# A local-attention stage on Trainium2: the mask moves from TensorE to VectorE, the output projection takes two tiles at a time, and the feed-forward moves between the halves of the weighing

## The chip, the cores and the metric

One Trainium2 chip, one of its cores. The metric is the device time of one execution of the whole program in microseconds; lower is better. The program runs nine phases one after the other. The change touches one of them, the local transformer, which takes from about 486 to 3685 us.

## The reference, cut to what matters

The input x is eight sequences of 512 tokens with 128 features. The local transformer has six layers, each an attention of 16 heads of 64 in windows of 32 keys with one window of look-back, and a gated feed-forward of 341 hidden units:

```
def local_attention(q, k, v):        # w = 32, bk2 = previous window and own window
    mask = (it < jb) | (it > jb + w) | (jb == -1)
    sim = jnp.einsum('bhwie,bhwje->bhwij', bq, bk2) * QK_SCALE
    sim = jnp.where(mask, -jnp.finfo(sim.dtype).max, sim)
    attn = jax.nn.softmax(sim, -1)
    out = jnp.einsum('bhwij,bhwje->bhwie', attn, bv2)
    return out.reshape(b, h, n, d)
...
    q = l2norm(q) * qs
    k = l2norm(k) * ksc
    q = q * cos * scale + rotate_half(q) * sin * scale
    k = k * cos * inv + rotate_half(k) * sin * inv
    return out @ Wo
...
for i in range(DEPTH):               # DEPTH = 6
    x = attn_layer(shift_tokens(x), Wqkv[i], q_scale[i], k_scale[i], Wo[i]) + x
    x = ffn_layer(shift_tokens(x), ln_g[i], ln_b[i], W1[i], b1[i], W2[i], b2[i]) + x
```

All is float32. Before this phase stands a gated delta rule; behind it follow a causal attention, a mixture of experts, a chunked attention, a second mixture of experts, another attention and a third mixture.

## The kernel before, in words

**Tiles.** A tile is 128 tokens; four tiles (t = k mod 4 = 0 to 3) are a sequence, 32 tiles a layer, 192 tiles the phase. Each engine has its own program in `local_transformer_phase`, unrolled in Python over `k` from -2 to 199, with semaphores counted per tile or per sequence; nothing is planned at run time, the order of the calls in each engine's loop is the order of the work. In iteration k the engines work on several tiles at once: the softmax and weighing of tile k, values and turned q and k of tile k+1, the q and k projections of tile k+2, the output of tile k-1.

**PE (loop at L1350).** make_scores(k): two bf16 matmuls write the mask into the two score banks (identity times `band8`, L1207), then 128 small matmuls of 64 rows and 32 columns add the scores on top (L1214). Then project_v (L1186 to L1188, three matmuls per 512 columns, float32 split in two parts), project_qk(k+2, 0), turn_out(k-1) (L1277), project_qk(k+2, 1), turn_probs(k) (L1253, waits for the exponentials), turn_qk(k+1) (L1266), weigh_values(k, 0), project_out(k-1) (L1304: eight 128x128 float32 products, each of two instructions in the trace), weigh_values(k, 1) (L1292, 64 small matmuls each half), and then the feed-forward's share: t = 0 ffn_a (L1342), t = 1 ffn_out (L1347) and ffn_turn (L1320), t = 3 ffn_gate (L1336). make_scores(k) waits for the first half of att of tile k-1 (`att_ready`).

**DVE (loop at L1674).** centre(k): maximum over each window from PSUM (L1605), subtraction of it from PSUM into `scores` (L1608). products(k+2): q and k times the rotary tables (L1618, four operations). sum_squares (L1624, one after the products and one after the first divide), ffn_shift at t = 2, divide(k, 0) and divide(k, 1) (L1630, L1634), between them add_output(k-1) (L1641). Then ffn_products at t = 0, ffn_add and ffn_stats at t = 1 (L1669, L1646 to L1653).

**ACT (loop at L1484).** invert_norms, copy_v, square(k+2, 0) (L1422), exponentials(k) (L1410), copy_out(k-1), square(k+2, 1), copy_probs, two copy_qk; scale_norm ahead of the square at t = 3, gelus with two table loads behind everything at t = 3.

**POOL (loop at L1560).** At t = 2 invert_deviation first (L1556, waits for the statistics); then normalise(k+1), two operations of 128x1024 with both inputs in SBUF (L1551), rotate(k+2), four of 128x512 (L1541), guard_norms.

**SP** issues the copies of the windows of v (window_values) and the weights of the next layer.

**PSUM** is full: scores and probabilities share banks 0 and 1, values, turned output and output projection (`WO_BANK`) banks 2 and 3, turned q and k banks 2 to 5, q and k 4 to 7, the feed-forward 6, 7 and 3. The waits `after_qk` and `ffn_banks_read` keep them apart.

## Time and profile before

| | us |
|---|---|
| median of 3 runs | 4785.16 |
| lowest and highest | 4783.14, 4789.26 |
| profiled execution | 4791.83 |
| its span, first to last instruction | 4789.8 |
| mean granted TensorE clock (share of full) | 0.927 |

Busy time of the whole span: PE 4238.3 us, the weight loads beside it (PEld) 3371.5, DVE 3247.4, ACT 2600.4, POOL 2418.3. Busy time says how long an engine had an instruction at work; on PE instructions overlap, so start-to-start times in the timeline are read rather than durations. In the timeline each line is one group of instructions alike: start, time, engine, line of the kernel, operation, what is written and read, the count, and in brackets how long the engine had been idle and who released it. "issue" means that the profile shows nothing that the engine waited for.

### The profile page before, as it was taken

Reading aid. Unit: us, or ns where it says so; the run is one execution under the profiler, and the core shown is the slowest. Engines: PE = TensorE matmul, PEld = TensorE weight load, DVE = VectorE, ACT = ScalarE, POOL = GpSimd, SP = SyncE. Lnnn points to the kernel's source line nnn. Section 1 sums busy time; section 2 is a strip of 40 time slices with the busy share of each in tenths; the row PEclk is TensorE's granted clock in tenths of the full one; section 3 lists DMA queues with packets and bytes.
Section 4 is the critical chain, followed back from the end, with each engine's and each line's share of the span. In section 5 each row is a group of like instructions: output and inputs, shape, how many; then the busy total and the mean of one; then the engine's idle time right before and its main releaser. Section 6 shows DMA issues by size and latency. Waiting matters only on the chain. (4 is left out here: it accounts for less than half of the span.)

```text
span 4789.8 us, 167679 instructions
## 1 busy us (share of the span) xinstructions
PE 4238.3 (88%) x70890; PEld 3371.5 (70%) x70890; DVE 3247.4 (68%) x5510; ACT 2600.4 (54%) x4233; POOL 2418.3 (50%) x1949
## 2 busy tenths in 40 slices
PE   6997899999999999999999999999997749658667
PEld 5885777777777777777777777777775439558447
DVE  4445777777777777777777777777775564564554
ACT  2231566665666666666666666666664317546435
POOL 2123655656565566555565666555652037516025
PEclk9777999999999999999999999999998959868878
DMA  0000322222222322222222222222221021222022
GB/s 25 0 0 30 88 67 65 64 80 67 69 67 62 86 66 69 64 80 69 69 64 80 68 64 70 64 69 69 69 64 36 0 61 50 67 61 62 7 63 75
DMA packets 214200, 281.53 MB, mean 59 GB/s; under 512 B 58878, under 2 KB 103716, under 8 KB 212740
## 3 DMA queue, kind: packets, MB, share of 16 engines
q1 hardware_dynamic: 203972, 251.85, 19.9%
q0 software_dynamic: 9536, 19.55, 1.5%
q8 instruction: 545, 8.93, 0.8%
q14 instruction: 147, 1.20, 0.1%
HBM read 54.88 MB, written 18.28 MB: 15 GB/s over the span
## 5 line engine op out<-in xcount | busy, mean ns | idle before, releaser
L1541 POOL TENSOR_TENSOR local_normed<-local_rot,local_sines 128x512 f32<-128x512 f32 x768 | 953.8, 1276 | 818.4 <-PE local_bank L1266 813.9
L1551 POOL TENSOR_TENSOR local_normed<-local_normed,local_inv_norm 128x1024 f32<-128x1024 f32 x384 | 732.8, 1929 | 276.1 <-ACT local_inv_norm L1441 276.1
L1618 DVE TENSOR_TENSOR local_rot<-local_bank,local_table 128x1024 f32<-128x1024 f32 x384 | 470.3, 1225 | 409.2 <-ACT local_squares L1422 402.6
L1186 PE MATMUL local_bank<-local_wqkv_hi,local_ys_hi 128*128 128x512 f32 x1152 | 496.8, 431 | 28.4 <-issue 17.4
L1417 ACT COPY local_v_tile<-local_bank 128x1024 f32<-128x1024 f32 x192 | 195.1, 1016 | 548.0 <-PE local_bank L1188 548.0
L1618 DVE TENSOR_TENSOR local_sines<-local_bank,local_table 128x1024 f32<-128x1024 f32 x384 | 466.4, 1215 | 0.0
L1624 DVE TENSOR_REDUCE local_norm<-local_squares 128x16 f32<-128x1024 f32 x384 | 464.0, 1209 | 0.0
L1188 PE MATMUL local_bank<-local_wqkv_hi,local_ys_lo 128*128 128x512 f32 x1152 | 458.8, 398 | 0.0
L1187 PE MATMUL local_bank<-local_wqkv_lo,local_ys_hi 128*128 128x512 f32 x1152 | 456.5, 396 | 0.0
L1422 ACT ACTIVATE local_squares<-local_bank 128x1024 f32<-128x1024 f32 x384 | 396.9, 1034 | 78.7 <-PE local_bank L1188 78.7
L1605 DVE TENSOR_REDUCE local_top<-local_bank 128x16 f32<-128x1024 f32 x192 | 234.8, 1223 | 246.2 <-PE local_bank L1214 245.8
L1304 PE MATMUL local_bank<-local_att_t,local_wo 128*128 128x128 f32 x3072 | 390.2, 280 | 4.3 <-ACT local_att_t L1446 1.2
L1304 PEld LDWEIGHTS local_bank<-local_att_t,local_wo 128*128 128x128 f32 x3072 | 358.6, 192 | 29.9 <-issue 9.9
L1266 PE MATMUL local_bank<-ident,local_normed 128*128 128x128 f32 x3072 | 373.7, 275 | 4.8 <-POOL local_normed L1551 4.1
L1292 PE MATMUL local_bank<-local_vals,local_probs_t 64*32 64x65 f32 x24576 | 348.2, 225 | 23.9 <-issue 20.6
L1266 PEld LDWEIGHTS local_bank<-ident,local_normed 128*128 128x128 f32 x3072 | 333.7, 142 | 24.5 <-POOL local_normed L1551 5.4
L1214 PEld LDWEIGHTS local_bank<-local_k_t,local_q_t 64*32 64x32 f32 x24576 | 256.7, 105 | 130.2 <-issue 129.9
L1292 PEld LDWEIGHTS local_bank<-local_vals,local_probs_t 64*32 64x32 f32 x24576 | 273.7, 105 | 90.7 <-issue 66.3
L1214 PE MATMUL local_bank<-local_k_t,local_q_t 64*32 64x64 f32 x24576 | 292.8, 225 | 43.9 <-issue 43.9
L1186 PEld LDWEIGHTS local_bank<-local_wqkv_hi,local_ys_hi 128*128 128x128 f32 x1152 | 220.6, 192 | 78.9 <-issue 30.7
L1634 DVE TENSOR_TENSOR local_att<-local_bank,local_inv_sum 128x512 f32<-128x512 f32 x384 | 265.5, 691 | 13.2
L1188 PEld LDWEIGHTS local_bank<-local_wqkv_hi,local_ys_lo 128*128 128x128 f32 x1152 | 220.2, 191 | 51.6
(421 smaller groups left out, 8957.0 us busy)
## 6 DMA issues: line engine op xcount, KB each, us to landing
local_vals<-local_v_tile SPq DMA_DIRECT2D x1152, 130.0 KB
local_vals<-local_v_tile SPq DMA_DIRECT2D x672, 65.0 KB
local_stage<-in_L_ffn_Wqkv SPq DMA_DIRECT2D x6, 1536.0 KB
moe_w<-y_rows SPq DMA_DIRECT2D x32, 256.0 KB, 4.9
moe_w<-in_L_ffn_W SPq DMA_DIRECT2D x3, 2048.0 KB, 9.9
x_rows<-moe_rows SPq DMA_DIRECT2D x12, 512.0 KB, 3.9
local_wo<-in_L_ffn_Wo SPq DMA_DIRECT2D x6, 512.0 KB, 9.0
moe_taken<-x_rows,moe_take POOLq DMA_INDIRECT x149, 2.6
```

Source lines behind the costliest of these rows:

```text
L1186: nc.tensor.matmul(out, hi, wqkv_hi[:, d0:d1], start=True, stop=False)
L1187: nc.tensor.matmul(out, hi, wqkv_lo[:, d0:d1], start=False, stop=False)
L1188: return nc.tensor.matmul(out, lo, wqkv_hi[:, d0:d1], start=False, stop=True)
L1214: last = nc.tensor.matmul(bank[b * BLOCK:(b + 1) * BLOCK, SCORES[odd], c * WIN:(c + 1) * WIN], q_t[rows, c, b * BLOCK:(b + 1) * BLOCK], k_ ...
L1266: last = nc.tensor.transpose(bank[:, QK_TURN[a][j // 4], j % 4 * P:(j % 4 + 1) * P], normed[:, (8 * a + j) * P:(8 * a + j + 1) * P], g.ide ...
L1292: last = nc.tensor.matmul(bank[b * BLOCK:(b + 1) * BLOCK, WEIGHED[i][odd], j * (HD + 1):(j + 1) * (HD + 1)], probs_t[rows, c, b * BLOCK:(b ...
L1304: last = nc.tensor.matmul(bank[:, WO_BANK, 0:P], wo[:, c, :], att_t[:, c, :], start=(c == 0), stop=(c == CH - 1))
L1422: nc.scalar.activation(squares[:, a * INNER:(a + 1) * INNER], two(QK[a]), ACT.Square).then_inc(q["squared"], 1)
L1541: last = nc.gpsimd.tensor_tensor(of_heads(normed, a)[:, :, to], of_heads(rot, a)[:, :, to], of_heads(sines, a)[:, :, of], ALU.add)
L1551: nc.gpsimd.tensor_tensor(of_heads(normed, a), of_heads(normed, a), inv_norm[:, a * HEADS:(a + 1) * HEADS].unsqueeze(2).to_broadcast([P, H ...
L1618: last = nc.vector.tensor_tensor(of_heads(out, a), src, table[:, m % TILES, row, :].unsqueeze(1).to_broadcast([P, HEADS, HD]), ALU.mult)
L1624: nc.vector.tensor_reduce(norm2[:, cols], of_heads(squares, a), AX, ALU.add).then_inc(q["norms_ready"], 1)
```

## The change

The two mask matmuls leave make_scores, and `band8` and `ident16` with them; the scores' matmuls start their own banks. centre adds the mask on VectorE while it copies the scores out of PSUM, takes the maximum from SBUF and subtracts in place. project_out runs in even iterations only, for the two tiles k-2 and k-1, with 256 moving columns; add_output likewise. `att_t` is twice as wide, and copy_out fills its half. PE's ffn_out, ffn_turn and ffn_gate move from behind weigh_values(k, 1) to before it, with a new wait `after_turn`; weigh_values(k, 1) comes behind them. Semaphore targets follow (`last_pair` is the last odd tile up to m, `wo_done` and `y_added` count two at once).

```diff
 def make_scores(m):
-    for odd in range(2):
-        nc.tensor.matmul(bank[:, SCORES[odd], :], ident16[:], band8[:, min(t, 1)].rearrange("p h k -> p (h k)"),
-                         start=True, stop=False, skip_group_check=True)
...
-                        start=False, stop=True, skip_group_check=True, tile_position=(HD * odd, b * BLOCK))
+                        start=True, stop=True, tile_position=(HD * odd, b * BLOCK))
 def project_v(m, k):
-    pe.wait_ge(q["y_added"], tile("y_added", k - 2))
+    pe.wait_ge(q["y_added"], tile("y_added", last_pair(k - 2)))
 def project_out(m):
-        last = nc.tensor.matmul(bank[:, WO_BANK, 0:P], wo[:, c, :], att_t[:, c, :], start=(c == 0), stop=(c == CH - 1))
-    last.then_inc(q["wo_done"], 1)
+        last = nc.tensor.matmul(bank[:, WO_BANK, 0:2 * P], wo[:, c, :], att_t[:, c, :], start=(c == 0), stop=(c == CH - 1))
+    last.then_inc(q["wo_done"], 2)
+def after_turn(k):
+    if is_tile(k + 1):
+        pe.wait_ge(q["qkt_copied"], tile("qkt_copied", k + 1, 1))
 def ffn_gate(n, k):
     after_qk(k)
+    after_turn(k)
 def ffn_out(n, k):
+    after_turn(k)
 # PE's loop
     if is_tile(k):
         weigh_values(k, 0)
-    if is_tile(k - 1):
+    if is_tile(k - 1) and k % 2 == 0:
         project_out(k - 1)
-    if is_tile(k):
-        weigh_values(k, 1)
-    if t == 0 and is_seq(n - 2):
-        ffn_a(n - 2, k)
     if t == 1 and is_seq(n - 2):
         ffn_out(n - 2, k)
     if t == 1 and is_seq(n - 1):
         ffn_turn(n - 1, k)
     if t == 3 and is_seq(n - 1):
         ffn_gate(n - 1, k)
+    if is_tile(k):
+        weigh_values(k, 1)
+    if t == 0 and is_seq(n - 2):
+        ffn_a(n - 2, k)
 # ACT
 def copy_out(m):
-    nc.scalar.copy(att_t[:].rearrange("p c t -> p (c t)"), two(OUT_TURN)).then_inc(q["out_copied"], 1)
+    nc.scalar.copy(att_t[:, :, m % 2 * P:(m % 2 + 1) * P], two(OUT_TURN).rearrange("p (c t) -> p c t", t=P)).then_inc(q["out_copied"], 1)
 # DVE
 def centre(m):
+    rows = scores[:].rearrange("p c a k -> p a c k")
     dve.wait_ge(q["scores_done"], tile("scores_done", m))
-    nc.vector.tensor_reduce(top[:], src, AX, ALU.max).then_inc(q["max_ready"], 1)
+    dve.wait_ge(q["probs_turned"], tile("probs_turned", m - 1))
+    nc.vector.tensor_tensor(rows, src, band[:, min(m % TILES, 1)].unsqueeze(1).unsqueeze(1).to_broadcast([P, 2, CH, WIN]),
+                            ALU.add).then_inc(q["masked"], 1)
+    dve.wait_ge(q["masked"], tile("masked", m))
+    nc.vector.tensor_reduce(top[:], rows, AX, ALU.max).then_inc(q["max_ready"], 1)
     dve.wait_ge(q["max_ready"], tile("max_ready", m))
-    dve.wait_ge(q["probs_turned"], tile("probs_turned", m - 1))
-    nc.vector.tensor_tensor(scores[:].rearrange("p c a k -> p a c k"), src, top[:].unsqueeze(3).to_broadcast([P, 2, CH, WIN]),
+    nc.vector.tensor_tensor(rows, rows, top[:].unsqueeze(3).to_broadcast([P, 2, CH, WIN]),
                             ALU.subtract).then_inc(q["centred"], 1)
 def add_output(m):
-    y = g.XH[:, s, c0:c0 + P]
-    nc.vector.tensor_tensor(y, bank[:, WO_BANK, 0:P], y, ALU.add).then_inc(q["y_added"], 1)
+    y = g.XH[:, s, c0:c0 + 2 * P]
+    nc.vector.tensor_tensor(y, bank[:, WO_BANK, 0:2 * P], y, ALU.add).then_inc(q["y_added"], 2)
```

## Rows read from the trace of the kernel before

**Rows 1.** The page: busy time by engine, and the instruction queue's packets and MB.
```profile
PE 4238.3 (88%) x70890; PEld 3371.5 (70%) x70890; DVE 3247.4 (68%) x5510; ACT 2600.4 (54%) x4233; POOL 2418.3 (50%) x1949
...
q8 instruction: 545, 8.93, 0.8%
```
**Rows 2.** Busy time by window: each engine's us and instructions, granted clock, DMA.
```profile
1700.00:2200.00 500.00, 482.26 (x9962) 374.71 (x9962) 382.65 (x511) 307.95 (x417) 300.87 (x236) 0.99 0.27 70
```
**Rows 3.** Timeline of PE, tile with t = 1, cut to its stations.
```profile
2220.15 0.59 PE L1207 MATMUL local_bank<-local_band,local_ident 128*128 128x512 bf16 x2
2220.68 1.48 PE L1214 MATMUL local_bank<-local_k_t,local_q_t 64*32 64x64 f32 x128
...
2227.24 1.04 PE L1253 MATMUL local_bank<-ident,local_scores 128*128 128x128 f32 x8
...
2230.03 0.86 PE L1292 MATMUL local_bank<-local_vals,local_probs_t 64*32 64x65 f32 x64
2230.90 2.02 PE L1304 MATMUL local_bank<-local_att_t,local_wo 128*128 128x128 f32 x16
2232.86 0.86 PE L1292 MATMUL local_bank<-local_vals,local_probs_t 64*32 64x65 f32 x64
2233.65 2.85 PE L1347 MATMUL local_bank<-local_gates,local_w 128*128 128x512 f32 x6
2236.42 0.46 PE L1320 MATMUL local_bank<-ident,XH 64*128 64x64 f32 x8
2236.82 0.61 PE L1207 MATMUL local_bank<-local_band,local_ident 128*128 128x512 bf16 x2
```
**Rows 4.** PE: starts of one sequence, its t = 3, the next; L1207 over the stage.
```profile
2203.84 0.59 PE L1207 MATMUL local_bank<-local_band,local_ident 128*128 128x512 bf16 x2
...
2250.80 0.59 PE L1207 MATMUL local_bank<-local_band,local_ident 128*128 128x512 bf16 x2 [0.40 <-DVE local_att L1634]
...
2268.08 0.59 PE L1207 MATMUL local_bank<-local_band,local_ident 128*128 128x512 bf16 x2
...
L1207 PE MATMUL local_bank<-local_band,local_ident x384: 376/379/391, 486.0 to 3635.7; 128*128 128x512 bf16 x192
```
**Rows 5.** Timeline of DVE in the same tile (t = 1) and into the next.
```profile
2222.20 1.23 DVE L1605 TENSOR_REDUCE local_top<-local_bank 128x16 f32<-128x1024 f32 x1 [1.03 <-PE local_bank L1214]
...
2226.20 1.22 DVE L1618 TENSOR_TENSOR local_rot<-local_bank,local_table 128x1024 f32<-128x1024 f32 x1 [1.52 <-ACT local_squares L1422]
...
2231.25 1.21 DVE L1624 TENSOR_REDUCE local_norm<-local_squares 128x16 f32<-128x1024 f32 x1
...
2236.53 0.75 DVE L1669 SCALAR_TENSOR_TENSOR XH<-local_bank,local_ln,XH 128x512 f32<-128x512 f32 x1 [1.07 <-PE local_bank L1347]
2237.61 0.87 DVE L1646 BATCH_NORM_STATS2 local_stats<-local_y_tok 128x6 f32<-128x128 f32 x4 [0.33 <-ACT local_y_tok L1452]
...
2239.01 1.22 DVE L1605 TENSOR_REDUCE local_top<-local_bank 128x16 f32<-128x1024 f32 x1
```
**Rows 6.** Timeline of ACT in the same tile: the square and the exponentials.
```profile
2225.14 1.03 ACT L1422 ACTIVATE local_squares<-local_bank 128x1024 f32<-128x1024 f32 x1 [0.35 <-PE local_bank L1188]
2226.06 1.05 ACT L1410 ACTIVATE local_scores<-local_scores 128x1024 f32<-128x1024 f32 x1
```
**Rows 7.** DVE's L1599 by its line (ns, least, median, most); POOL's timeline at t = 2.
```profile
L1599 DVE TENSOR_TENSOR local_wqkv_lo<-local_stage,local_wqkv_hi x18: 1214/2919/2922, 460.4 to 3117.0; 128x1024 fp32r<-128x1024 f32 x18
...
2239.18 1.04 POOL L1556 TENSOR_TENSOR local_rstd<-local_var_eps,minus_half 128x4 f32<-128x4 f32 x1 [1.97 <-DVE local_var_eps L1653]
2240.19 3.77 POOL L1551 TENSOR_TENSOR local_normed<-local_normed,local_inv_norm 128x1024 f32<-128x1024 f32 x2
```
**Rows 8.** PE's waits, 700 to 3500 us: total us, times, longest.
```profile
PE local_bank L1214 <- issue: 34.8, 22, 2.1
```
**Rows 9.** Timeline of PE: stops in the scores, first tiles and one at t = 3.
```profile
502.87 0.31 PE L1214 MATMUL local_bank<-local_k_t,local_q_t 64*32 64x64 f32 x5 [1.55 <-issue]
...
562.92 0.63 PE L1214 MATMUL local_bank<-local_k_t,local_q_t 64*32 64x64 f32 x37 [1.42 <-issue]
...
2319.56 0.27 PE L1214 MATMUL local_bank<-local_k_t,local_q_t 64*32 64x64 f32 x2 [1.76 <-issue]
```
**Rows 10.** Busy time by window behind that stop; the clock is third from the end.
```profile
2315.00:2325.00 10.00, 7.83 (x183) 6.03 (x179) 5.25 (x7) 3.88 (x9) 5.08 (x4) 0.83 0.03 8
```

More of the change, by code:

```diff
@@ L1024, in body @@
         band = sb("band", [P, 2, WIN])
-        band8 = sb("band8", [P, 2, CH, WIN], BF16)
-        ident16 = sb("ident16", [P, P], BF16)
         squares = sb("squares", [P, 2 * INNER])
@@ L1043, in body @@
         att = sb("att", [P, INNER])
-        att_t = sb("att_t", [P, CH, P])
+        att_t = sb("att_t", [P, CH, 2 * P])
         y_tok = sb("y_tok", [P, TOKENS])
@@ L1058, in body @@
                     "exp_done": 1, "v_copied": 1, "squared": 2, "probs_t_ready": 1, "qkt_copied": 2, "out_copied": 1,
-                    "max_ready": 1, "centred": 1, "qk_normed": 2, "products_ready": 2, "norms_ready": 2,
+                    "masked": 1, "max_ready": 1, "centred": 1, "qk_normed": 2, "products_ready": 2, "norms_ready": 2,
                     "sums_inverted": 2, "att_ready": 2, "y_added": 1,
@@ L1075, in body @@
                     "logs_ready", "inv_norms_ready")
-        DVE_MADE = ("max_ready", "centred", "products_ready", "norms_ready", "sums_inverted", "att_ready", "y_added",
+        DVE_MADE = ("masked", "max_ready", "centred", "products_ready", "norms_ready", "sums_inverted", "att_ready", "y_added",
                     "stats_ready", "aggregated", "var_ready", "shift_ready", "prod_ready", "seq_done")
@@ L1104, in is_seq, with last_pair @@
             return 0 <= n < RUNS
+        def last_pair(m):
+            return m if m % 2 else m - 1
         def two(banks):
@@ L1181, in _ @@
                 credit(pe, PE_MADE)
-                pe.wait_ge(pads_ready, 2)
+                pe.wait_ge(pads_ready, 1)
                 def product(out, hi, lo, d0, d1):
@@ L1273, in turn_out @@
                     else:
-                        pe.wait_ge(q["y_added"], tile("y_added", m - 1))
+                        pe.wait_ge(q["y_added"], tile("y_added", last_pair(m - 1)))
                         ffn_banks_read(k - 1, (3,))
@@ L1297, in project_out @@
                 def project_out(m):
-                    if m % PER_LAYER == 0:
+                    if m % PER_LAYER == 1:
                         pe.wait_ge(wo_loaded, 16 * (m // PER_LAYER + 1))
@@ L1444, in copy_out @@
                     act.wait_ge(q["out_turned"], tile("out_turned", m))
-                    act.wait_ge(q["wo_done"], tile("wo_done", m - 1))
-                    nc.scalar.copy(att_t[:].rearrange("p c t -> p (c t)"), two(OUT_TURN)).then_inc(q["out_copied"], 1)
+                    act.wait_ge(q["wo_done"], tile("wo_done", last_pair(m - 1)))
+                    nc.scalar.copy(att_t[:, :, m % 2 * P:(m % 2 + 1) * P], two(OUT_TURN).rearrange("p (c t) -> p c t", t=P)).then_inc(q["out_copied"], 1)
                 def copy_turned(n):
@@ L1478, in _ @@
                 nc.scalar.preload_act_table_set("natural_log_exp_and_others")
-                act.wait_ge(pads_ready, 2)
+                act.wait_ge(pads_ready, 1)
                 for part in range(3):
@@ L1581, in _ @@
                 dve.wait_ge(consts_loaded, CONST_LOADS)
-                nc.vector.tensor_copy(ident16[:], g.ident[:])
-                nc.vector.tensor_copy(band8[:], band[:].unsqueeze(2).to_broadcast([P, 2, CH, WIN])).then_inc(pads_ready, 1)
                 def scale_tables(layer):
@@ L1637, in add_output @@
                 def add_output(m):
-                    s, c0 = m // TILES % SEQS, m % TILES * P
+                    s, c0 = m // TILES % SEQS, (m - 1) % TILES * P
                     dve.wait_ge(q["wo_done"], tile("wo_done", m))
-                    y = g.XH[:, s, c0:c0 + P]
-                    nc.vector.tensor_tensor(y, bank[:, WO_BANK, 0:P], y, ALU.add).then_inc(q["y_added"], 1)
+                    y = g.XH[:, s, c0:c0 + 2 * P]
+                    nc.vector.tensor_tensor(y, bank[:, WO_BANK, 0:2 * P], y, ALU.add).then_inc(q["y_added"], 2)
                 def ffn_stats(n):
@@ L1687, in _ @@
                         sum_squares(k + 2, 1)
-                    if is_tile(k - 1):
+                    if is_tile(k - 1) and k % 2 == 0:
                         add_output(k - 1)
```

## The prediction

> **What bounds the kernel now.** I read the page first: PE is the busiest engine, 88% of the span [rows 1]. The busy share by windows then shows the stage that the diff touches, the local transformer (about 486 to 3685 us, 192 tiles): PE 482 of 500 us, DVE 383, ACT 308, POOL 301 [rows 2]. The timeline of PE shows one tile as an unbroken run: mask 0.53 us (start to start), scores 1.41, projections and the turned output to 6.56 after the scores' start, then the turned probabilities, the turned q and k, the first half of the weighing at 9.35, project_out 1.96, the second half 0.79, then the feed-forward's share of that tile [rows 3]. Four tiles (t = 0 to 3) make one sequence: the one shown takes 64.24 us [rows 4], and I take 63.9 for one with no stop at all. Over the stage the mask's line gives the mean: 3149.7 us for 191 tiles, 65.96 a sequence [rows 4]. PE waits for another engine at one place in each sequence, 0.40 us for DVE's att ahead of t = 3 [rows 4]. So PE's order sets the time, and whoever is late with the softmax comes next.
>
> I write S for the start of a tile's scores (2220.68). From [rows 5, 6]: DVE begins the max at S+1.52 and has centred at S+4.0; ACT does a square at S+4.46 and only then the exponentials at S+5.38, which end as PE reaches turn_probs (S+6.56). The centring has 1.4 us of slack, turn_probs has none.
>
> **What the change takes from PE.**
> Mask: 4 x 0.53 = 2.1 us a sequence; the scores' own 128 products stay [rows 3].
> project_out: two tiles took 2 x 1.96 = 3.92. The new form has 16 instructions of 256 columns for the pair. Those of 512 columns start every 0.45 us (2.77 us for 6, L1347) and those of 128 every 0.12 (1.96 for 16) [rows 3], so 256 lies near 0.22 and the pair near 3.5. Bounds: 3.9 (no gain at all) and 2.0 (as dear as one tile was). I take 3.5, nearest to half the 512 form: 0.8 us a sequence.
> Wait for att: the odd tiles get the feed-forward between the halves, the even ones 3.5 us of projection, so att's first half has over 1 us of slack: 0.4 us goes.
> Sum on PE alone: 63.9 - 3.3 = 60.6 us a sequence. (The two DVE operations that made the bf16 tables once, before the loop, go as well: under 2 us, left out.)
>
> **What it adds.**
> (a) The add is one 128x1024 VectorE operation. No such row from PSUM plus a table exists except L1618 (1.22, PSUM times a table) [rows 5]: 1.25 us with its gap, bounds 1.1 and 1.9. The max then reads SBUF, as L1624 does in 1.21. If DVE is free, centring ends at S+5.25 instead of 4.0, and the exponentials can't start before S+5.38 anyway. So the add costs nothing in a tile where DVE is free and alone; each us later than that is one us of PE.
> (b) The subtraction now has both inputs in SBUF. The row for that is L1599, 1.21 us at least and 2.92 at the median of 18 [rows 7]: it is the same size, and its long cases lie beside POOL's normalising (L1551, 1.9 each). The difference, 1.7, is nearly one POOL operation. So I price a meeting by what is left of POOL's running operation, 0 to 1.9 us. (The Trainium skill, "SBUF — State Buffer", section "Who interferes with whom", says that a VectorE instruction with two SBUF inputs contends with a GpSimd instruction that reads SBUF, that the loser is fully blocked, and that a reduce never contends; the trace agrees with the first part by 2.92 against 1.21. By the rule the new max is safe and the subtraction is not.)
> (c) t = 2. During t = 1 DVE has, after the second att, ffn_add and the statistics: L1669, L1646 and their small followers take 0.67 + 1.40 us to the next max [rows 5]. PE's t = 1 is now only 9.35 + 0.88 + 2.77 + 0.40 + 0.83 = 14.2 us (it was 16.67, with mask and project_out in it). DVE: the first norm sum at S+10.57 [rows 5] plus 1.13, att 0.84, second sum 1.13: 13.7; it waits for the second half of the weighing to 14.35; att to 15.2, ffn_add 15.9, statistics 17.25. PE's scores of t = 2 start at 14.2 and DVE would be wanted at 15.7: 1.5 us late. POOL's deviation and normalising follow the statistics (1.01 us apart) [rows 7]: 18.4 to 20.3 for the first half; the subtraction comes at 19.75 and waits 0.55. Exponentials 2.0 us late, PE idle 2.0 us ahead of turn_probs of t = 2. Bounds: 1.5 (no meeting) and 3.4 (a whole POOL operation).
> (d) Other tiles. t = 3: the normalising is in its second half when the subtraction comes, 0.65 us, hidden by the 0.6 that scale_norm puts ahead of the exponentials there. t = 0: 0.2. t = 1: POOL is done by then, 0.
> (e) ffn_gate stands 0.88 us after the start of the weighing and waits for products_ready of the tile after next (after_qk); the products end about 0.5 us later: 0.5 us in t = 3. Behind it the second half of the weighing waits too. ffn_turn has ffn_out's 2.77 us as cover and waits for nothing. SP's queue is not reordered; its window copies hang on pv_done of the second half, now up to 1.2 us later in odd tiles after the first, needed a tile later. ACT's gelus start earlier, their table loads lie in the gap that was idle.
> Result: t = 0 17.3 + 0.2, t = 1 14.2, t = 2 14.6 + 2.0, t = 3 14.3 + 0.5, together 63.1 against 63.9: only 0.8 of the 3.3 us is left, 46 sequences x 0.8 = 37 us.
>
> (f) The stop for instructions. Twenty-two times in the stage PE stops inside the scores for "issue", 34.8 us in all [rows 8]. The page has 545 packets on the instruction queue for 141,780 PE and PEld instructions: about 260 each [rows 1]. By counting instructions along the timeline, the stops lie a multiple of 256 apart. In the steady state all are at t = 3, and only where such a boundary lies in the second half of the scores: t = 3 is the one tile whose scores come right after 64 weighing products, with no feed-forward (12 slow instructions in 2.7 us) between. The first tiles, which have none either, stop in each of five: 1.55, 0.45, 1.64, 0.18 and 1.42 us, mean 1.05 (first and last of them shown) [rows 9]. After the change the scores come right behind the second half of the weighing in three of four tiles, and the mask's 0.53 us between is gone. At t = 2 DVE is 1.5 us late anyway and hides most of it. At t = 3 and t = 0: 2 x (1.05 + 0.3 for the lost mask at half the boundaries) = 2.7 us a sequence, against 34.8/43 = 0.8 now: 1.9 more, 87 us. Bounds: 0 (other lateness takes them in) and 3.2 a sequence (2.4 us, the longest kind, at half the boundaries of all three, less what DVE hides).
> (g) After 8 of those 22 stops the granted clock fell: a stretch of 10 us shows 0.83 [rows 10] and eight matmuls at 0.43 instead of 0.23 us; that is about 1.8 us each. Twice the stops: 0.35 a sequence, 16 us. Bounds 0 and 50.
> (h) Five layer boundaries, where the DVE is behind by its weight splits: 1.25 to 3 us each, 8 us.
>
> **Sum.** -37 + 87 + 16 + 8 = +74 us. The profiled execution took 4791.8 us (span 4789.8), so 4866 for its like; its median sister runs are 6.7 us lower, 4785.2, so I forecast 4859.
>
> **Rivals.**
> B, the stops don't multiply: boundaries still come, but the other waits of the new order cover them. For it: they are absent in every tile with a feed-forward between, so the queue refills in under 3 us. Against it: the stops of the first tiles [rows 9]. Time: 4785 - 37 + 8 = 4756; with project_out at its best, about 4700. This is the case on the other side, and the point where it decides is whether "issue" ahead of the scores stays near 35 us; up to about 70 us it still comes out level or faster.
> C, PE stays the bound and DVE's additions are hidden at t = 2 too (statistics earlier than I set them, no meeting with POOL): 4785 - 46 x 3.3 = 4633, and up to 4700 with the 0.5 of ffn_gate and some stops. Against it: DVE's work in t = 1 alone adds up to more than PE's tile.
> D, stops at full price in all three tiles and the clock falls after many of them and after the 2 us waits of t = 2: 87 becomes 147, 16 becomes 50: 4785 - 37 + 147 + 50 + 8 = 4953.
> That project_out gains nothing would move each of these by 46 x 0.8 = 37 us and is in the ranges. The change does what it says in all of them: the mask's lines can't be hidden work on PE.
>
> **How the numbers follow.** Forecast 0.42 (4800 to 4910), B 0.22, C 0.14, D 0.22. The likeliest is 4859. The range leaves out the lower half of C and the far end of D: 4690 to 4950. A measurement of this kernel can tell about 0.2% (10 us) from no change. Faster: C and most of B, 0.34; within 0.2%: the seam between B and the forecast, 0.06; slower 0.60.
>
> **What would show it.** Right: no L1207 matmul; the pair's projection at 3.4 to 3.6 us per 16 instructions; VectorE's add at 1.2; the subtraction with a median near 1.2 and a tail to 3 us; PE waiting some 2 us for ACT's scores ahead of turn_probs in every fourth tile; "issue" ahead of the scores' products over 100 us. Wrong: "issue" unchanged (then B), turn_probs never waiting (then C), or the mean sequence under 65 us.

## The result, and the profile after

The changed kernel takes 4842.99 us (median of 4 runs, 4836.72 to 4844.17), the kernel before 4787.21 beside it: ratio 1.0107, 95% interval 1.0089 to 1.0125, so 1.1% slower. The profiled execution has a span of 4842.4 us against 4789.8. In the local stage the scores of the first and of the last of its 192 tiles start at 483.7 and 3686.7 us, 3203.0 us apart; in before they start at 486.5 and 3636.0, 3149.5 apart. So the whole difference of the spans, 52.6 us, lies in that stage.

The page of after, the share by windows (as [rows 2]) and PE's waits from 700 to 3500 us (total us, times, longest; as [rows 8]):

```profile
PE 4138.4 (85%) x68970; PEld 3281.9 (68%) x68970; DVE 3574.1 (74%) x5604; ACT 2599.8 (54%) x4233; POOL 2453.6 (51%) x1949
...
q8 instruction: 530, 8.68, 0.8%
```

```profile
1700.00:2200.00 500.00, 460.05 (x9607) 354.94 (x9592) 430.25 (x521) 299.81 (x406) 300.22 (x233) 0.99 0.25 67
```

```profile
PE local_bank L1213 <- issue: 90.8, 58, 2.4
PE local_bank L1252 <- ACT local_scores L1416: 48.9, 51, 3.1
PE local_bank L1341 <- DVE local_sines L1625: 25.9, 40, 0.7
PE local_bank L1188 <- issue: 20.9, 10, 4.0
PE local_bank L1276 <- ACT local_v_tile L1423: 11.8, 22, 1.0
```

PE has 100 us less work over the span and yet fills only 460 of 500 us, where it filled 482. What it saves it spends waiting: for instructions inside the scores (90.8 us, 34.8 before), for the exponentials ahead of the turned probabilities (48.9, 4.0 before), and ahead of ffn_gate for the products (25.9, none before). Two waits of before are gone: stops for instructions inside the weighing (18.0 us) and the wait for att (9.9). The same view of before, behind the 34.8 us of [rows 8]:

```profile
PE local_bank L1292 <- issue: 18.0, 43, 1.6
...
PE local_bank L1207 <- DVE local_att L1634: 9.9, 25, 0.4
PE local_bank L1253 <- ACT local_scores L1410: 4.0, 5, 0.9
```

PE's timeline, two tiles with t = 0 and what stands between, cut to its stations (as [rows 3, 4]):

```profile
2161.30 1.26 PE L1213 MATMUL local_bank<-local_k_t,local_q_t 64*32 64x64 f32 x105
2163.97 0.42 PE L1213 MATMUL local_bank<-local_k_t,local_q_t 64*32 64x64 f32 x23 [1.41 <-issue]
...
2169.47 1.03 PE L1252 MATMUL local_bank<-ident,local_scores 128*128 128x128 f32 x8
...
2173.14 3.69 PE L1303 MATMUL local_bank<-local_att_t,local_wo 128*128 128x256 f32 x16
2176.76 0.86 PE L1291 MATMUL local_bank<-local_vals,local_probs_t 64*32 64x65 f32 x64
2177.55 2.84 PE L1347 MATMUL local_bank<-local_xn,local_w 128*128 128x512 f32 x6
2180.32 1.49 PE L1213 MATMUL local_bank<-local_k_t,local_q_t 64*32 64x64 f32 x128
...
2194.32 1.08 PE L1213 MATMUL local_bank<-local_k_t,local_q_t 64*32 64x64 f32 x87
2197.49 0.66 PE L1213 MATMUL local_bank<-local_k_t,local_q_t 64*32 64x64 f32 x41 [2.08 <-issue]
...
2224.24 2.81 PE L1341 MATMUL local_bank<-local_xn,local_w 128*128 128x512 f32 x6 [0.65 <-DVE local_sines L1625]
2226.99 0.86 PE L1291 MATMUL local_bank<-local_vals,local_probs_t 64*32 64x65 f32 x64
2227.64 1.01 PE L1213 MATMUL local_bank<-local_k_t,local_q_t 64*32 64x64 f32 x79
2229.20 0.73 PE L1213 MATMUL local_bank<-local_k_t,local_q_t 64*32 64x64 f32 x49 [0.55 <-issue]
...
2235.72 1.09 PE L1252 MATMUL local_bank<-ident,local_scores 128*128 128x128 f32 x8 [0.54 <-ACT local_scores L1416]
...
2246.64 1.48 PE L1213 MATMUL local_bank<-local_k_t,local_q_t 64*32 64x64 f32 x128
```

Look at the two t = 0 tiles. The first stops for 1.41 us and then doesn't wait for the exponentials; the second stops for 0.55 and waits 0.54. They take 19.02 us (2161.30 to 2180.32) and 19.00 (2227.64 to 2246.64). The stop and the late softmax lie in the same stretch, and the tile takes as long as the longer of them asks. Why the softmax is late there is on the other engines, DVE and then POOL and ACT, in the second of these tiles:

```profile
2229.97 1.23 DVE L1610 TENSOR_TENSOR local_scores<-local_bank,local_band 128x1024 f32<-128x1024 f32 x1 [1.15 <-PE local_bank L1213]
2231.23 1.22 DVE L1613 TENSOR_REDUCE local_top<-local_scores 128x16 f32<-128x1024 f32 x1
2232.48 2.09 DVE L1615 TENSOR_TENSOR local_scores<-local_scores,local_top 128x1024 f32<-128x1024 f32 x1
```

```profile
2229.72 3.77 POOL L1557 TENSOR_TENSOR local_normed<-local_normed,local_inv_norm 128x1024 f32<-128x1024 f32 x2 [2.23 <-ACT local_inv_norm L1447]
```

```profile
2234.61 1.06 ACT L1416 ACTIVATE local_scores<-local_scores 128x1024 f32<-128x1024 f32 x1 [0.66 <-DVE local_scores L1615]
```

The add and the maximum take 1.23 and 1.22 us. The subtraction takes 2.09. It starts 0.9 us after the second of POOL's two operations has started and ends 1.08 us after that one has ended (2234.57 and 2233.49). In a t = 0 tile without a stop (scores from 2296.00) it starts 0.15 us into the second operation, takes 2.83, and ends 1.07 after it:

```profile
2300.09 2.83 DVE L1615 TENSOR_TENSOR local_scores<-local_scores,local_top 128x1024 f32<-128x1024 f32 x1
```

```profile
2298.08 3.77 POOL L1557 TENSOR_TENSOR local_normed<-local_normed,local_inv_norm 128x1024 f32<-128x1024 f32 x2 [2.23 <-ACT local_inv_norm L1447]
```

In the tile with the stop of 1.41 us it starts 1.75 us into the second operation and takes 1.24, and ends 1.08 us after it too. So POOL's end sets the subtraction's end, whether PE has stopped for 0, 0.55 or 1.41 us, and that is how a stop hides. From the third sequence on the t = 0 tiles with stops up to 1.4 us take 18.97 to 19.30 us, as those without one do; the eight with stops above 1.8 us take 19.63 to 21.67. The line over all tiles (ns: least, median, most) shows the meeting as the prediction set it out, one of 1.2 us alone and up to 3.0 when it waits:

```profile
L1615 DVE TENSOR_TENSOR local_scores<-local_scores,local_top x192: 1224/1227/2970, 488.3 to 3692.4; 128x1024 f32<-128x1024 f32 x192
```

Length of a tile, from the start of its scores (in before of its mask) to the next (us; from the third sequence on, layer boundaries left out). "Least" is the shortest tile, one without a stop for instructions; I call such tiles quiet. It can hold other waits:

| t | before, least / mean | predicted without stops | after, least / mean |
|---|---|---|---|
| 0 | 16.17 / 16.35 | 17.5 | 18.97 / 19.28 |
| 1 | 16.67 / 16.87 | 14.2 | 13.97 / 14.02 |
| 2 | 13.96 / 14.08 | 16.6 | 16.39 / 16.97 |
| 3 | 16.79 / 18.31 | 14.8 | 14.87 / 16.07 |
| sum | 63.6 / 65.6 | 63.1 | 64.2 / 66.3 |

With the boundaries a sequence takes 67.16 us in the mean against 66.27.

### The profile page after: what moved, and what is told of

Same layout as the page of the kernel before. It is cut to its first block and busy times, and to the rows that moved or that the text cites. A ratio compares the mean times of both kernels' runs of the same rounds, so it can differ in the third digit from the quotient of the medians.

```text
span 4842.4 us, 163981 instructions
## 1 busy us (share of the span) xinstructions
PE 4138.4 (85%) x68970; PEld 3281.9 (68%) x68970; DVE 3574.1 (74%) x5604; ACT 2599.8 (54%) x4233; POOL 2453.6 (51%) x1949
## 3 DMA queue, kind: packets, MB, share of 16 engines
q14 instruction: 149, 1.22, 0.1%
## 5 line engine op out<-in xcount | busy, mean ns | idle before, releaser
L1557 POOL TENSOR_TENSOR local_normed<-local_normed,local_inv_norm 128x1024 f32<-128x1024 f32 x384 | 767.9, 2021 | 169.5 <-ACT local_inv_norm L1447 169.5
L1625 DVE TENSOR_TENSOR local_rot<-local_bank,local_table 128x1024 f32<-128x1024 f32 x384 | 469.5, 1223 | 185.9 <-ACT local_squares L1428 179.0
L1213 PE MATMUL local_bank<-local_k_t,local_q_t 64*32 64x64 f32 x24576 | 307.2, 226 | 112.7 <-issue 108.6
L1265 PE MATMUL local_bank<-ident,local_normed 128*128 128x128 f32 x3072 | 378.6, 277 | 5.0 <-POOL local_normed L1557 4.1
L1213 PEld LDWEIGHTS local_bank<-local_k_t,local_q_t 64*32 64x32 f32 x24576 | 268.4, 105 | 158.2 <-issue 156.0
L1303 PE MATMUL local_bank<-local_att_t,local_wo 128*128 128x256 f32 x1536 | 354.9, 384 | 2.6 <-ACT local_att_t L1452 1.1
L1265 PEld LDWEIGHTS local_bank<-ident,local_normed 128*128 128x128 f32 x3072 | 338.6, 143 | 25.4 <-POOL local_normed L1557 5.6
L1610 DVE TENSOR_TENSOR local_scores<-local_bank,local_band 128x1024 f32<-128x1024 f32 x192 | 235.0, 1224 | 155.1 <-PE local_bank L1213 154.7
L1291 PE MATMUL local_bank<-local_vals,local_probs_t 64*32 64x65 f32 x24576 | 332.7, 225 | 5.5 <-issue 2.2
L1615 DVE TENSOR_TENSOR local_scores<-local_scores,local_top 128x1024 f32<-128x1024 f32 x192 | 314.6, 1638 | 6.6
L1303 PEld LDWEIGHTS local_bank<-local_att_t,local_wo 128*128 128x128 f32 x1536 | 283.9, 190 | 50.2 <-issue 1.7
```

Of the source, the lines that this page charges most:

```text
L1213: last = nc.tensor.matmul(bank[b * BLOCK:(b + 1) * BLOCK, SCORES[odd], c * WIN:(c + 1) * WIN], q_t[rows, c, b * BLOCK:(b + 1) * BLOCK], k_ ...
L1265: last = nc.tensor.transpose(bank[:, QK_TURN[a][j // 4], j % 4 * P:(j % 4 + 1) * P], normed[:, (8 * a + j) * P:(8 * a + j + 1) * P], g.ide ...
L1291: last = nc.tensor.matmul(bank[b * BLOCK:(b + 1) * BLOCK, WEIGHED[i][odd], j * (HD + 1):(j + 1) * (HD + 1)], probs_t[rows, c, b * BLOCK:(b ...
L1303: last = nc.tensor.matmul(bank[:, WO_BANK, 0:2 * P], wo[:, c, :], att_t[:, c, :], start=(c == 0), stop=(c == CH - 1))
L1557: nc.gpsimd.tensor_tensor(of_heads(normed, a), of_heads(normed, a), inv_norm[:, a * HEADS:(a + 1) * HEADS].unsqueeze(2).to_broadcast([P, H ...
L1625: last = nc.vector.tensor_tensor(of_heads(out, a), src, table[:, m % TILES, row, :].unsqueeze(1).to_broadcast([P, HEADS, HD]), ALU.mult)
```

## The experiments

They ran on three chips (e1 to e4, e5 to e8, e9 to e12), each time with the kernel before beside them. On the first of these chips the kernel before takes 4900 us, on the others 4791, so each kernel is given as its ratio to before on its own chip, and set against 1.0107 for after, which was not run again on them. The profiled executions allow a second comparison. Behind the last tile's scores 1263 to 1269 us follow on the chip of e1 to e4 and 1149 to 1164 on the others, so that chip is slower behind the stage. The stage itself, first to last tile's scores, takes 3149.5 us in before, 3203.0 in after, 3148.9 in e1, 3202.1 in e2, 3279.3 in e3, 3144.4 in e4, 3218.3 in e5 and 3153.6 in e6: the same picture as the ratios, to within 0.3% of the time.

**e1, the mask back on TensorE** (pair and new order kept):

```
-  dve: rows = src + band;  top = max(rows);  rows = rows - top
+  pe:  for odd in range(2): matmul(bank[:, SCORES[odd], :], ident16, band8[:, min(t, 1)], start=True, stop=False)
+  dve: top = max(src);  rows = src - top
```

> The changed kernel with the mask back on TensorE (two bf16 matmuls ahead of the scores) and the maximum and subtraction reading PSUM again; pair projection and new order stay. Theory (late softmax at t = 0 and t = 2 from VectorE's add and the meeting with POOL, plus more stops for instructions): PE gets 2.1 us a sequence back to do, but both lates go and the 0.53 us gap returns; near 4785 us, waits of turn_probs for ACT under 5 us, stops in the scores still some 60. Rival (the new order and its stops alone cost the time, the add is free): not faster than the changed kernel, 4845 to 4940 us, since PE only gets more work.

Measured: 1.0018 (1.0009 to 1.0028). Nearly the whole loss is gone. Least lengths 17.92, 14.63, 15.24 and 15.54: t = 0 and t = 2 win 1.1 us each, t = 1 and t = 3 lose 0.7 each. PE's waits:

```profile
PE local_bank L1218 <- issue: 60.5, 55, 1.7
PE local_bank L1346 <- DVE local_sines L1629: 27.5, 42, 0.7
...
PE local_bank L1257 <- ACT local_scores L1421: 3.9, 5, 0.8
```

The wait for the exponentials goes from 48.9 to 3.9 us. The stops are nearly as many (55 for 58), but 1.1 us each instead of 1.6, shorter by about the 0.53 us that the mask's two products take between the weighing and the scores.

**e2, the old order** (feed-forward's pieces again behind the second half of the weighing; mask and pair as in after):

```
-                    if t == 1: ffn_out, ffn_turn;  if t == 3: ffn_gate
                     weigh_values(k, 1)
+                    if t == 1: ffn_out, ffn_turn;  if t == 3: ffn_gate
```

> The changed kernel with ffn_out, ffn_turn and ffn_gate behind the second half of the weighing again. Theory: only t = 3 has its scores right behind the weighing, so stops in the scores fall from 60 to about 22; the 0.65 us waits of ffn_gate for VectorE's products go; VectorE is still late at t = 2 and meets POOL at t = 0. Near 4800 us. Rival (order is harmless, the add on VectorE is all of the loss): same as the changed kernel, 4843, stops unchanged.

Measured: 1.0123 (1.0106 to 1.014), no better than after. Near 4800 us were expected, hardly any loss; that was a miss:

```profile
PE local_bank L1291 <- ACT local_k_t L1440: 69.9, 84, 0.8
PE local_bank L1252 <- ACT local_scores L1416: 42.1, 73, 2.2
PE local_bank L1213 <- issue: 34.2, 25, 2.3
PE local_bank L1291 <- issue: 33.9, 30, 1.6
```

The stops in the scores fall to 34.2 us, what before had. But in the odd tiles, which have no projection any more, the second half of the weighing now stands right behind the first and waits 0.8 us for ACT's copy of k, and stops for instructions itself. The new order is what fills the place that the pairing left empty; the two edits belong together, and undoing one of them shows a wait that neither before nor after has.

**e3, one tile's projection at a time** (mask and order as in after):

```
-                    if is_tile(k - 1) and k % 2 == 0: project_out(k - 1)      # 256 columns
+                    if is_tile(k - 1):                project_out(k - 1)      # 128 columns
```

> The changed kernel with one tile of output projection per iteration again (128 moving columns). Theory: PE does 0.3 to 0.8 us more a sequence, but t = 1 gets 1.96 us longer and VectorE's statistics are done in time for t = 2, so the lateness there shrinks from 1.9 to at most a meeting: 4800 to 4850 us, about the same as the changed kernel. Rival (pairing is a plain gain of PE time, nothing hangs on it): 4843 + 37 = 4880.

Measured: 1.0252 (1.0235 to 1.0269), 1.4% over after, beyond both expectations. So the pairing is worth about 1.5 us a sequence, not 0.8. PE's own part is smaller than that: the pair starts at 2173.14 and the next block at 2176.76, so it takes 3.62 us against 2 x 1.96 [rows 3], which is 0.6 a sequence. The medians of t = 1 and t = 3 lose 1.8 and 2.3 us, while t = 0 and t = 2 win back only 1.3 and 1.1 of the 1.66 (3.62 - 1.96) that their shorter projection saves. What holds these two back was not followed to its end.

**e4, the maxima in PSUM**, so that the subtraction has one input in SBUF:

```
+                    top = bank[:, PROBS[0], 0:2 * CH].rearrange("p (a c) -> p a c", c=CH)
-                    nc.vector.tensor_reduce(top[:], rows, AX, ALU.max)        # top: a tensor in SBUF
+                    nc.vector.tensor_reduce(top, rows, AX, ALU.max)
```

> The changed kernel with the window maxima written to PSUM (bank 0, free once the add has read the scores), so that the subtraction has one SBUF input only; the same computation. Theory: the subtraction takes 1.22 us in every tile (mean now 1.64), POOL's normalising 1.90 (now 2.02); t = 0 falls from 19.0 to near 17.3 us where no stop falls into it, t = 2 by 0.5; about 4790 us. Rival (the subtraction's long times are waits that cost nothing, because stops and statistics are late anyway): 4835 to 4845, same as the changed kernel.

Measured: 1.0021 (1.0009 to 1.0034), 0.9% below after. The subtraction's line and PE's waits:

```profile
L1615 DVE TENSOR_TENSOR local_scores<-local_scores,local_bank x192: 1220/1220/1223, 491.1 to 3637.6; 128x1024 f32<-128x1024 f32 x192
```

```profile
PE local_bank L1212 <- issue: 94.1, 62, 2.2
...
PE local_bank L1251 <- ACT local_scores L1415: 17.2, 20, 2.1
```

The same 128x1024 operation at the same places takes 1220 ns each of 192 times; the least t = 0 tile falls from 18.97 to 17.52 us, which is what was predicted for it. POOL's normalising gains too: 2024 ns in the mean of after, 1932 before, 1934 here. (The Trainium skill, "SBUF — State Buffer", section "Who interferes with whom", has it so: one SBUF input doesn't contend with GpSimd, two do, and the reduce never does. The trace agrees: beside POOL the subtraction took up to 2970 ns with two SBUF inputs and at most 1223 with one, and the reduce from SBUF at most 1223 in after.)

**e5, the statistics later**: ffn_stats behind the softmax's three operations in t = 2 instead of ahead of them, and the deviation behind POOL's normalising.

```
                     if is_tile(k): centre(k)
+                    if t == 2: ffn_stats(n - 1)
...
-                    if t == 1: ffn_stats(n - 1)
```

> After, with the statistics of the feed-forward's normalisation issued behind the centring on VectorE in t=2, and the deviation's inverse behind the normalisation on the other engine, so that t=2's maximum and subtraction no longer stand behind them. Theory (the softmax of t=2 is late because VectorE does the statistics first): t=2 falls from 16.4 us to about 14.6 to 15.0, the time to some 1% below after (ratio to before near 1.002 instead of 1.0107). Rival (t=2 is late because the maximum waits for the scores themselves and the subtraction meets POOL, the statistics only fill idle time): t=2 stays within 0.3 us and the time within 0.2% of after.

Measured: 1.015 (1.0132 to 1.0168), if anything slower than after. The theory fell; the least t = 2 tile stays at 16.3 (16.4 in after).

```profile
PE local_bank L1213 <- issue: 93.7, 57, 2.6
PE local_bank L1265 <- DVE local_sines L1625: 27.2, 37, 1.0
...
PE local_bank L1252 <- ACT local_scores L1416: 21.0, 35, 1.9
```

The wait for the exponentials falls by 27.9 us and a new one of 27.2 us stands one step on: the statistics (1.4 us) now lie between the softmax and the products of q and k, and the turned q and k (L1265) wait for those. In this order DVE does the same work in t = 2, and another instruction waits for it.

**e6, e4 and e5 together** (the two diffs above):

> Both repairs together: maxima in PSUM (as in e4, which took 0.9% off after) and the statistics behind the centring (as in e5). If the two latenesses are separate terms, quiet tiles go to about 17.5, 14.0, 14.7 and 14.9 us = 61.1 a sequence against 64.3 in after, but stops for instructions that the late softmax hid become visible in t=0 and t=2; so ratio to before 0.985 to 0.995. If the stops take all of what the late softmax gave, it is as e4, 1.002.

Measured: 1.0037 (1.0023 to 1.0051): as e4 or slightly above, the lower of the two expectations. The least sequence is 61.9 us (64.5 in after), 0.8 above the 61.1 that the expectation added up. With the meeting gone the statistics' new place does help the least t = 2 tile: 15.37, for 15.99 in e4. But the mean is 66.2, 4.3 above the least sequence, with 95.2 us of stops: little is left in which a stop could hide.

**e7 and e8, where the stops fall.** Counted along the trace, a sequence of after has 2612 PE instructions (matmuls, weight loads and the sequencer's own), 10 x 256 + 52 (2614 where a layer begins). All 69 stops in the scores of after, and all 30 of before, lie at an instruction whose number leaves the same rest by 256: 28 or 29, counted from the first PE instruction of the trace (the expectations count from another start, with 198). So the boundary moves 52 instructions (26 matmuls) from one sequence to the next, and after five sequences is back. Both kernels are e6 with 204 empty instructions (semaphore increments) a sequence; they differ only in how many stand once ahead of the loop:

```
+                for _ in range(160):          # e8: 50
+                    pe.sem_inc(padding, 1)
...
+                    pad(k, 0)                 # 80 in t = 2, 124 in t = 3
```

> e6 with 204 empty instructions a sequence in TensorE's program (80 in t=2, 124 in t=3, in groups of about 30 between blocks) and 160 once ahead, so that a sequence has 2816 = 11 x 256 instructions and every multiple of 256 (counted from instruction 198) falls at matmul 20 to 38 of the scores in t=0, 2 and 3, or behind a wait. Theory (a stop comes only where a boundary falls late in a run of small matmuls right behind the weighing): the 60 stops of 1.6 us go to nearly none, 94 us less of idle time, against which stand the empty instructions themselves. Ratio to before 0.97 to 0.985. Rival (the stops come from something else, such as the queue of the instruction transfers): as many stops as in e6.

> As e7, with 50 instead of 160 empty instructions once ahead, so that the boundary falls at matmul 93, 75 and 92 of 128 in the scores of t=0, t=2 and t=3 of every sequence. The same instructions a sequence. Theory: a stop of 1.4 to 2.4 us in three tiles of each of 46 sequences, 110 to 140 stops, 150 to 250 us more idle time and 100 to 220 us slower than e7 (some of it hidden where the softmax is late anyway). Rival (position tells nothing): e7 and e8 agree within 0.2%.

Measured: 1.1571 (1.1552 to 1.159) and 1.1885 (1.1865 to 1.1905), 5544.31 and 5687.98 us. The empty instructions cost far more than they could win: in e7 t = 2 and t = 3 last 22.7 and 25.3 us at least, against 15.4 and 14.9 in e6, and the mean of the two grows by 80 ns for each empty instruction. The lower granted clock is in that figure: 0.90 from 700 to 3500 us, in e7 as in e8, for 0.99 in e6. The row of e7 (as [rows 2]), and PE's idle time, which stands where the groups of empty instructions stand:

```profile
700.00:3500.00 2800.00, 2281.97 (x44050) 1754.78 (x44049) 1919.51 (x2367) 1422.20 (x1897) 1353.21 (x1063) 0.90 0.23 57
```

```profile
PE local_bank L1188 <- issue: 188.3, 69, 3.3
PE local_bank L1276 <- issue: 174.0, 69, 3.4
```

As a remedy it failed. As a test it holds, for e7 and e8 have the same instructions a sequence and the same clock: from 700 to 3500 us e7 has not one stop in its scores, e8 has these (e7's answer has no such line):

```profile
PE local_bank L1213 <- issue: 124.8, 80, 2.3
```

and e8 is 143.7 us slower, inside the 100 to 220 expected.

**e9 and e10, the same with small matmuls as filling**, on e4:

```
                     (turn_out, ahead of the transposes)
+                    for _ in range(39 if m == 0 else {1: 25, 2: 26}.get(m % TILES, 0)):        # e10: 10
+                        nc.tensor.matmul(bank[0:BLOCK, OUT_TURN[0], 0:WIN], g.ident[0:HD, 0:BLOCK], g.ident[0:HD, 0:WIN],
+                                         start=True, stop=True, tile_position=(0, 0))
```

> e4 (the maxima in PSUM) with 51 small float32 matmuls a sequence (204 instructions: 25 ahead of t=2's transposes of the attention's output, 26 ahead of t=3's, into a bank that the transposes then overwrite) in place of e7's empty instructions, and 39 once in the first tile. A sequence has 2816 = 11 x 256 instructions, and the boundaries fall at matmul 36 to 40, 20 to 22 and 26 to 29 of the scores in t=0, 2 and 3. A scores matmul takes 11.5 ns, two per float32 call, so the filling costs 51 x 23 ns = 1.2 us a sequence. Theory (position decides): no stops in the scores, quiet tiles as e4's best ones, about 17.6, 14.0, 15.9 and 15.4 us = 62.9, a mean near 64.0 with the layer boundaries against 65.95 in e4; ratio to before 0.975 to 0.99. Rival (stops come as often, or elsewhere in the tile): ratio 1.00 to 1.01.

> The same as e9 with 10 in place of 39 fillers in the first tile: the boundaries fall at matmul 98, 80 and 87 of the scores in t=0, 2 and 3 of every sequence. Theory: some 130 stops of 1.6 us; t=2 and t=3 longer by about 1.6 us each, t=0 by 1.0 to 1.6, 3 to 5 us a sequence: slower than e9 by 150 to 220 us. Rival: equal to e9 within 0.2%.

Measured: 1.0212 (1.0196 to 1.0228) and 1.0638 (1.0622 to 1.0653), 4894.97 and 5098.42 us. The difference of 203.5 us, 4.2% of the time, comes from 29 calls (58 small matmuls) fewer in one tile; 150 to 220 were expected. PE's waits in e10, and one of its scores:

```profile
PE local_bank L1212 <- issue: 169.1, 108, 2.2
```

```profile
2246.42 1.15 PE L1212 MATMUL local_bank<-local_k_t,local_q_t 64*32 64x64 f32 x95
2249.18 0.46 PE L1212 MATMUL local_bank<-local_k_t,local_q_t 64*32 64x64 f32 x33 [1.61 <-issue]
```

In e9 no line for the scores is left in that view; its sequences inside a layer take 66.8 to 68.0 us, where those of e6 take 61.9 to 69.0. In e10 the stops of t = 0, 2 and 3 come after 98, 80 and 88 of the 128 matmuls in the first layer and one matmul earlier with each layer. They last 1.83, 1.38 and 1.21 us in the mean of the 47, 40 and 47 tiles that stop, 198 us over the span, for 203.5 us of time: with the softmax on time a stop costs about its length.

That e9 itself lost to e4 is the price of the filling. One line of its timeline:

```profile
2240.16 2.95 PE L1275 MATMUL local_bank<-ident 64*32 64x64 f32 x50
```

It is 59 ns a matmul, not the 11.5 of the scores (1.47 us for 128) that I had reckoned with: 6.0 us a sequence instead of 1.2. The scores go in turn to eight tile positions of the array, the filling always to one, and always into the same place of PSUM; which of the two makes it slow no run tells. So the 1.9% between e9 and e4 is filling, less the stops. An estimate from these rows, not run: with fillers of 11.5 ns e9 would be 4.8 x 46 = 221 us shorter, less some 70 us of waits in t = 2 and t = 3 that the filling covers now (18.0 - 2.95 and 17.3 - 3.09 are 0.9 and 0.65 below the least tiles of e4), which would be near 0.99 of before.

**e11, e1 with filling (47 instead of 51), and e12, after with the filling of e9:**

> e1 (mask added by TensorE, the pair of tiles and the new order kept) with 47 fillers a sequence so that it too has 2816 instructions and its boundaries fall at matmul 38, 16 and 25 of the scores. Its stops were 62.6 us in 57, and shorter, for the mask's matmuls split the run. Theory: they go, 1.1 us a sequence of filling comes: ratio to before 0.985 to 0.997 against 1.0018 in e1. It tells, against e9, what the mask on VectorE costs once the subtraction has its maxima from PSUM: the theory of the prediction (TensorE's 2.1 us a sequence less against late softmaxes) lets e9 win by 0 to 1%.

> After itself with the 51 fillers a sequence of e9. The stops of after cost 94 us of idle time, of which the trace shows t=0's and t=2's as hidden by the late softmax. Theory: only t=3's 24 to 30 us and some of t=2's come back, and the filling costs 55 us less what t=3's wait for the products hides: ratio to before 1.003 to 1.010, so better than after (1.0107) by 0 to 0.8%. Rival (all 94 us were exposed): 0.995 to 1.000.

Measured: 1.0351 (1.0335 to 1.0367) and 1.0325 (1.0311 to 1.034); both expectations missed by the filling's price. Among themselves e9, e11 and e12 have no stops in the scores, so they show the rest undisturbed. e12 to e9 is the meeting alone: 1.0325 to 1.0212, 1.1%, all in t = 0 (18.99 against 17.53 at least, 19.03 against 17.95 in the mean). e12 has the wait, e9 has no such line:

```profile
PE local_bank L1252 <- ACT local_scores L1419: 29.4, 41, 1.0
```

And e12's t = 0 tiles, which have no stops, take 19.03 us in the mean, those of after, which have, 19.28: of 31 us of stops there only some 11 were paid (0.25 us in each of 46 sequences). e11 to e9 is the mask: without stops and without the meeting, its move to VectorE wins 1.3%, though e9 has four calls of filling (0.5 us) a sequence more.

In e9 one wait is left in t = 0, which after has as well (11.8 us in 22, t = 2 included):

```profile
PE local_bank L1278 <- ACT local_v_tile L1425: 17.3, 32, 1.0
```

PE waits there for ACT's copy of v. In after ACT itself waits ahead of that copy for the transfer of the window of v, 51.4 us in 33 tiles from 700 to 3500 us, which it never did in before.

## Why the prediction was right, and where it was not

The forecast was 4859 us for a median of 4843, with the right sign and inside its own range of 4800 to 4910. Of its mechanism the list of what happens is right: the mask off PE, a late softmax in t = 2, a meeting with POOL, more stops for instructions. The sum is not. Two large errors of opposite sign stand in it: the quiet tiles were set 65 us too short over the stage, stops and clock some 97 us too dear (d and f below). That the total came within 16 us is luck.

**PE's gain: right in kind.** The mask's line is gone and the least t = 1 tile is 13.97 us (14.2 predicted). The pair takes 3.62 us, just above the 3.4 to 3.6 that was to show it; 0.6 us a sequence by that row instead of 0.8. e3 adds that the pairing is worth 1.5 in the whole.

**(a) right.** The add takes 1.22 us and costs nothing in t = 1.

**(b) right.** Shown by e4: the same subtraction with its maxima in PSUM never meets POOL.

**(c) t = 2, right in size.** 16.39 us against 16.6. Both reasons given are at work, but they don't add up one by one: the meeting out of the way brings 0.4 us (e4, 15.99), the statistics out of the way alone nothing (e5, 16.30), both together 1.0 (e6, 15.37). What is left above the 14.6 of a tile without lateness, 0.8 us, no run explains.

**(d) t = 0, a step that failed.** Predicted 17.3 + 0.2, measured 18.97. The meeting was set at 0.2 us, as if the subtraction came at the end of a POOL operation. In the tiles without a stop it comes when the second has just begun (0.15 us) and loses 1.6 us (2.83 for 1.22). The tile loses 1.1 us in the mean (e12 against e9) and 1.45 in the least ones (after against e4). That is the mis-sized term: the least tiles sum to 64.2 us, not 63.1. Those of before sum to 63.6, and its least whole sequence is 63.9, where after's is 64.5. Like against like a quiet sequence loses 0.6 us instead of winning 0.8: +28 us over 46 sequences in place of -37.

**(e) right for ffn_gate**, which waits 0.65 us in the 40 of t = 3 that wait (0.5 predicted). The copies of the windows of v, "needed a tile later" and priced at nothing, do cost: e9, where no softmax is late, shows 17.3 us of waiting for them. In after such a wait comes ahead of the late softmax in the same tile (1.0 us in the tile from 2296.00), so most of it should hide there; no run tells the two apart.

**(f) the stops, right in the profile and wrong in the time.** 90.8 us are in the window for 34.8 before, and over the whole span they are 108.6 (over 100 predicted) for 43.9. But +87 us of time was put beside it. The mean of a sequence lies above the sum of the least tiles by 2.0 us in before and by 2.1 in after, +6 us in all, clock included. The failed step is "other lateness takes them in": it was kept as the lower bound, and applied to t = 2 alone. In t = 0 the subtraction's meeting makes the softmax late as well. From the third sequence on, 31 us of stops stand in t = 0, where the mean lies 0.3 us (14 us in all) above the least tile, and 34 us in t = 2, where it lies 0.6 above it (27 us). t = 3 has stops in both kernels. And the stops inside the weighing, 18.0 us in before, are gone in after; the prediction counted only those in the scores. e10 shows what stops cost when nothing is late: 198 us of them for 203.5 us. So (d) and (f) are one error: a softmax later than thought, which cost more itself and hid more of the stops.

**(g) small, as said.** From 700 to 3560 us, projection instructions of 0.55 us and more, those at the lower clock, are 119 of 3072 against 70 of 3096; at 0.2 us each that is 10 us, 16 predicted. They are already in the +6 of (f). **(h)** A sequence with a layer boundary takes 7.4 us more than one inside a layer, 6.1 in before: 6 us for five of them, 8 predicted.

In all: 28 + 6 + 6 = +40 us over 46 sequences; some 13 more fall in the first two sequences and the last three tiles. Together that is the 53.5 us measured for the stage, where +74 was predicted.

**The rivals.** B fell by its own mark, "issue" near 35 us, yet its idea (other waits cover the stops) holds for t = 0. C fell by the waits for the exponentials. D's condition, stops in all three tiles at full price, is nearly e10: possible, but not with 2612 instructions to a sequence, where the boundary moves on by 52 each time.

No kernel run here beats the one before. e1 and e4, at 1.0018 and 1.0021, come within 0.2% of it by different ways: e1 gives PE its mask back and so takes DVE out of the path; e4 keeps PE's gain and then pays for stops.

## What to carry to other kernels

Work taken off the bound engine is worth only what the next one can deliver: list for each tile when its operands are ready on the new engine, and look at the whole load of that engine there, since moving one of its operations only moves the wait. Two latenesses that end at the same instruction don't add up; price the longer. When a stop recurs at a fixed number of instructions, count the instructions of a loop's round modulo that number before adding or removing any: it decides which stretch the stop falls in.

## What the runs showed of the hardware

- PE's stops in the scores lie at a boundary that comes every 256 instructions: 69 of 69 in after, 30 of 30 in before. The page's 530 packets of q8 for 137,940 PE and PEld instructions are 260 each.
- Not every boundary in the scores stops PE. In after the stops come after 59 or more of the 128 matmuls; those after 87 and more last 1.4 to 2.4 us, those earlier 0.3 to 2.1. In t = 1, where a block of 512-column matmuls stands right ahead, there are none (one of 3.7 us in the first sequence, which has no such block yet).
- A few matmuls decide the size. In e10 the stops of t = 3 last 1.6 to 2.2 us where they come after 86 to 88 matmuls, and 0.2 to 0.9 after 83 or 84.
- Where PE's boundary fell was worth 203.5 us in one program of 4895 (e9 and e10).
- A matmul of 64x32 by 64 columns takes 11.5 ns in turns over eight tile positions and 59 ns repeated at one position and into one place of PSUM (e9).
- An empty semaphore instruction on PE cost about 80 ns in e7, at a granted clock of 0.90.
- With its maxima in PSUM instead of SBUF a subtraction that has POOL beside it took 1220 ns each time, instead of up to 2970; the maximum itself took 1228 ns instead of 1220.
- The subtraction with both inputs in SBUF waits out POOL's operation whole: 102 of the 192 in after started while one of POOL's normalising operations (1.9 us) ran, from 0.11 to 1.89 us into it, and 95 of them ended 1.08 us after it had ended.
